# First attention's loop: SyncE issues the next output weights' loads and the kept operands' write in front of the second stacking

## The reference, cut to what matters

```
x = x + 0.5 * ffn(layernorm(x))          # router, top 2 of 8 experts of rank 16
x = x + attention(layernorm(x))          # latent attention, 32 heads
x = x + 0.5 * ffn(layernorm(x))
```

```
q = rms_norm(x @ wq_a.T, q_norm_w) @ wq_b.T        # 128 plain + 64 rotated columns a head
kv = x @ wkv_a.T                                   # 128 latent + 64 rotated, shared by the heads
kv_up = rms_norm(kv_c, kv_norm_w) @ wkv_b.T        # k_nope and v of each head
scores = (q_nope . k_nope + q_pe . k_pe) * scale   # causal
out = softmax(scores) @ v                          # all heads, then out @ wo.T
```

## Time and profile before

| | |
|---|---|
| median of 3 timed runs | 2177.68 us (2177.6 to 2181.52) |
| profiled execution | 2180.48 us |
| its span, first to last instruction | 2178.7 us |
| granted TensorE clock, mean | 0.998 |
| PE busy | 2123.7 us (97%) |
| DVE, ACT, POOL busy | 1585.4, 1371.0, 1247.1 us (73%, 63%, 57%) |
| iteration of the first attention's loop | 60.1 us |
| queue q1 | 244.64 MB, 36.7% of 16 engines' span |

### The profile page before, as it was taken

The page is one execution under the profiler, slowest core; times in us unless marked ns, Lnnn a source line. Parts: engine busy times, 40 slices in busy tenths (PEclk is TensorE's granted clock), DMA queues, the critical chain, the costliest instruction groups (busy, mean ns, idle before and its releaser), DMA issues.

```text
span 2178.7 us, 44641 instructions
## 1 busy us (share of the span) xinstructions
PE 2123.7 (97%) x11548; PEld 1802.3 (83%) x11548; DVE 1585.4 (73%) x3415; ACT 1371.0 (63%) x3561; POOL 1247.1 (57%) x1643
## 2 busy tenths in 40 slices
PE   8989999999999999999899999999999999999998
PEld 7977888888888888888688978888888888888877
DVE  7667777777777777778787667777777777777777
ACT  6556666666666666666665566666666666666664
POOL 5336666666776666666554355555555555555543
PEclk9999999999999999999999999999999999999999
DMA  4034444443334444445423133333333333333331
GB/s 164 19 79 142 137 146 136 145 127 120 104 119 138 146 135 142 146 155 165 147 79 121 52 101 115 114 114 114 114 114 114 114 114 114 114 114 114 111 98 78
DMA packets 221201, 258.02 MB, mean 118 GB/s; under 512 B 145872, under 2 KB 174672, under 8 KB 219088
## 3 DMA queue, kind: packets, MB, share of 16 engines
q1 hardware_dynamic: 216528, 244.64, 36.7%
q10 hardware_dynamic: 4608, 12.58, 1.7%
HBM read 127.14 MB, written 79.69 MB: 95 GB/s over the span
## 4 chain that ended last, share of the span: by engine, by line
PE 65%; DMA 10%; POOL 9%; issue 5%; DVE 4%; ACT 3%; SPq 3%; POOLq 0%; ACTq 0%; DVEq 0%
PE ps L890 50%; DMA stage<-in_wo 7%; PE ps L969 5%; PE ps L1302 4%; PE ps L1246 2%; DMA arena<-arena 2%; PE ps L916 1%; DMA stage<-stage 1%; POOL arena L2703 1%; PE ps L904 1%; SPq L781 1%; POOL stage L2704 1%; POOL stage L2698 1%; ACT arena L1463 1%; ACT stage L1837 1%
## 5 line engine op out<-in xcount | busy, mean ns | idle before, releaser
L2412 DVE TENSOR_TENSOR xacc<-ps,xacc 128x512 f32<-128x512 f32 x896 | 603.0, 686 | 190.9 <-PE ps L890 177.1
L2021 DVE TENSOR_TENSOR arena<-ps,arena 128x512 fp32r<-128x512 f32 (+4 forms) x744 | 425.3, 577 | 202.0 <-ACT arena L1463 201.7
L890 PE MATMUL ps<-arena,extra 128*128 128x512 f32 x1920 | 522.6, 401 | 5.7 <-DVE xacc L2412 5.4
L1828 ACT ACTIVATE stage<-ps,negmax 128x128 f32<-128x128 f32 (+6 forms) x512 | 260.2, 508 | 339.3 <-DVE negmax L2391 332.7
L1463 ACT ACTIVATE arena<-ps 128x512 fp32r<-128x512 f32 (+4 forms) x744 | 369.3, 506 | 137.9 <-PE ps L890 57.3
L890 PE MATMUL ps<-zT,arena 128*128 128x512 f32 (+1 forms) x1746 | 446.3, 400 | 1.9 <-DVE arena L2021 1.0
L890 PEld LDWEIGHTS ps<-arena,extra 128*128 128x128 f32 x1920 | 341.7, 188 | 88.8 <-DVE xacc L2412 17.9
L890 PEld LDWEIGHTS ps<-zT,arena 128*128 128x128 f32 x1746 | 317.6, 189 | 68.8 <-ACT stage L1463 1.3
L2716 POOL TENSOR_TENSOR extra<-extra_plain,extra 128x256 fp32r<-128x256 f32 (+1 forms) x256 | 223.4, 875 | 164.8 <-ACT extra L1463 164.4
L890 PE MATMUL ps<-arena 128*128 128x512 f32 x960 | 262.1, 408 | 14.2 <-POOL arena L2716 7.9
L890 PE MATMUL ps<-keyT,arena 128*128 128x192 f32 (+5 forms) x1152 | 265.7, 339 | 3.6 <-ACT stage L1828 3.6
(11 more groups left out here) (129 smaller groups left out, 3117.9 us busy)
## 6 DMA issues: line engine op xcount, KB each, us to landing
kept_b<-arena SPq DMA_DIRECT2D x16, 3584.0 KB, 11.2
arena<-kept_b SPq DMA_DIRECT2D x112, 512.0 KB, 6.1
arena<-arena SPq DMA_DIRECT2D x128, 128.0 KB, 3.0
stage<-in_wo SPq DMA_DIRECT2D x32, 512.0 KB, 13.2
stage<-stage SPq DMA_DIRECT2D x248, 64.0 KB, 2.0
extra<-arena SPq DMA_DIRECT2D x120, 128.0 KB, 3.0
kept_q<-arena SPq DMA_DIRECT2D x16, 768.0 KB, 11.1
arena<-kept_q ACTq DMA_DIRECT2D x32, 384.0 KB, 6.6
```

What stands on the lines that cost most here:

```text
L890: last = nc.tensor.matmul(dst, w, m, start=start and n == 0, stop=stop and n == len(passes) - 1, skip_group_check=skip)
L1828: nc.scalar.activation(prob[u][:, poff(u, i):poff(u, i) + w], bank_s(i)[:, 0:w], ACT.Exp, bias=negmax[:, k % 2, i:i + 1], accum_out=rowsum ...
L2021: return nc.vector.tensor_tensor(dst, src, part.bitcast(F32), ALU.subtract)
L2412: nc.vector.tensor_tensor(xs, bank_y(k, j), xs, ALU.add).then_inc(y_added, 1)
```

## The change

Inside `body`, in the first attention (p = 0), the block of four moves from behind the second stacking to a place in front of it, directly behind the swap for `pe0`; in the block, `load_wo(g + 1)` moves in front of `kept(g - 1)` and `keep_b(g)`. In the groups with early loads the fourth early load now comes behind the block. The last group's `kept(g)` stays at the end. Nothing is computed in another way, and `first_body` and the second attention stay as they are.

```diff
                     swap_halves()
+                if p == 0 and not last:
+                    landed_wqn(g + 1)
+                if p == 0:
+                    split_b(g)
+                    if not last:
+                        load_wo(g + 1)
+                    kept(g - 1)
+                    keep_b(g)
                 if early:
                     load_early(g, 3)
                 if not last:
                     stack_halves(turns(p, g, 1) + 1, 0, 4 * slot_n(p, g, 2))
-                if p == 0:
-                    if not last:
-                        landed_wqn(g + 1)
-                    split_b(g)
-                    kept(g - 1)
-                    keep_b(g)
-                    if not last:
-                        load_wo(g + 1)
-                    else:
-                        kept(g)
+                if p == 0 and last:
+                    kept(g)
```

## The result

The changed kernel takes 2187.26 us (median of 6 runs, 2184.82 to 2190.23) against 2178.82 us of the kernel before (6 runs): a ratio of 1.0039, 95% interval 1.0027 to 1.0052. It is slower by 8.4 us, 5.9 to 11.3 by the interval. A second set, beside its parts, gave 2189.49 against 2179.79, 1.0041 (1.0028 to 1.0054). I had forecast a slower kernel, by 5 us. The median of the kernel before stands at 2178.82 with six runs, where the forecast started from the 2177.68 of three.

What follows compares the result with a forecast made beforehand. TensorE, busy 97%, was taken as the bound; 13 x (0.9 - 0.75) = +2.0, next to last iteration +2.05, last +1 gave +5 us: 2182.7 against 2177.68, with 8 in 10 from 2168 to 2194.

Steps and rivals of the forecast that it cites:

- The bound and the old stop: TensorE, 97% busy, stops 0.75 us per iteration for the output weights; removing this gives -10.5 us.
- The number of old stops: Stops of TensorE at the output weights' products: 14 taken as removed, -10.5 us together (bounds -6.7 and -12.7).
- When the block starts: On SyncE, first DMA at 705.9, 0.3 us after DVE's last low part; through by 709.1, stacking's issue not delayed.
- The loads: Output weights on SyncE's queue: asked for 10.3 us earlier, landing in 4.1 to 5.3 us, by 713; wanted at 729.
- The stacking behind write and loads: Stacking transfers land at 723.75, after the next first scores want them; TensorE stops 0.9 us (bounds 0.25 and 1.25).
- the first body's order: First body's loads, stacking, then write take 17.2 us together; from 705.9 that ends at 723.1.
- the loop's sum: In the loop, write and loads need 15.3 us, stacking alone 2.9; together 18.2 us, ending at 724.1.
- The early groups: Last two iterations with early loads of x: +2.05 us in the next to last, +1 in the last.
- What moved along: After the stacking, GpSimd's 2.72 us wait for the swap shrinks and it starts 2 to 3 us earlier; counted as nothing.
- The stop moves and nothing is left: Rival: stacking lands at 723.1, -3.5 us, 2174; chance 0.15, including a stop just as long as the old one.
- Faster: Rival: stacking passes or shares engines with the write, landing before 722.85; -10.5 us, 2167; chance 0.22.
- Clearly slower: Rival: write at loop pace and slower 256 B pieces, stacking landing at 724.5; 2193 us; chance 0.18.

Runs made afterwards that it cites:

- the other two executions: Profiled executions of the changed kernel again (2189.49 us) and of the change in groups 1 to 13 only (2184.18 us), with periods 60.59 and 60.46 us.
- the loop alone: The change in groups 1 to 13 only, groups with early loads of x in the old order: 2184.18 us against 2180.05 of the kernel before, ratio 1.0022.
- the early groups alone: The change in groups 14 and 15 only, groups 1 to 13 in the old order: 2184.89 us against 2179.79 of the kernel before, ratio 1.0020.

## Why the prediction was right

- **The bound and the old stop.** 0.75 us was worked out from the gap (0.48), the overlap (0.16) and the longer first product (0.11). The periods give 0.77. The weight port's 12.7 us over 14 alone would have said 0.91, the array's 6.7 over 14 would have said 0.48.
- **The number of old stops: one too many.** Of the 14 of the earlier trace rows one stands in group 0, ahead of the loop, and group 15 didn't wait for its output weights before. 13 stops were removed, so the removed term is 13 x 0.75 = 9.75 us and not 10.5, and the next to last iteration's term should have been 2.8, without the 0.75 taken off.
- **When the block starts.** 0.3 us after the low part, and the stacking's issue still on time: both as stated.
- **The loads.** They land in 4.4 to 6.3 us for the 4.1 to 5.3 reckoned. The stop at line 1246 is gone.
- **The stacking behind write and loads: the right mechanism, a term sized too small.** Taken 0.9 us, measured 1.18 by the periods; between the bounds 0.25 and 1.25. I had put the landing midway between the first body's order (17.2 us from the first issue) and the loop's sum (18.2). In the iteration shown this came true: it landed 17.83 us after the first issue (711.33 to 729.16) for the 17.85 taken, and the scores began 18.26 us after the low part where they begin 17.41 after it in the kernel before (705.58 to 722.99), 0.85 us late for the 0.9. As idle time of the array that is 0.71, since the overlap of 0.16, which the stop takes away, doesn't show in it. But this is one of the shorter gaps. The longest and the shortest of the 13:

```profile
245.28 0.39 PE L1280 MATMUL ps<-keyT,arena 128*128 128x256 f32 x1 [1.21 <-DMA arena<-arena]
426.66 0.38 PE L1280 MATMUL ps<-keyT,arena 128*128 128x256 f32 x1 [0.54 <-DMA arena<-arena]
```

Their mean is 12.1/13 = 0.93, so the landing is on average 0.2 us later than I took, nearer to the loop's sum. The other 0.1 us is a term that I had counted in the old stop and left out of the new one: the first product behind a stop takes 0.38 us for 0.28. 0.93 + 0.16 + 0.10 = 1.19. The same sum with the mean gap of the other two executions (1.00 and 0.88) gives 1.26 and 1.14 where their periods give 1.26 and 1.13. With 1.18 the 13 groups cost 13 x (1.18 - 0.77) = 5.3 us instead of 2.0.
- **The early groups: about the right size, in part by another path.** Forecast +3.05. The whole less the loop alone is 3.1 us by the medians, the early groups alone 5.1. DVE's wait was put at 3.4 us and was 3.72; in group 15 it was put at 1 and was 0.67. PE's stop of 2.8 us was to be a wait for the late stacking; it was a wait for DVE at line 890, of 2.26 us, and the stacking landed within it. That the sum still fits is in part luck: the forecast had too long a stop there and took a stop off it that didn't exist.
- **What moved along.** GpSimd's wait for the first swap fell from 2.72 us to 0.34, as expected, for nothing:

```profile
678.40 1.27 POOL L2698 TENSOR_TENSOR stage<-stage,pos_tab 128x512 f32<-128x512 f32 x1 [0.34 <-POOL stage L2693]
```

- **Not foreseen:** the issues of the stacking grow from 2.7 to 10 us. It cost next to nothing: with six sevenths of the write in front the issue still took 9.1 us and 0.12 us of the stop were left. SyncE waits for the landing anyway.
- **The rivals.** "The stop moves and nothing is left" took the first body's 17.2 us for the loop; the loop is nearer 18. "Faster" took a place in the queue for harmless. It holds for each half of the block alone, where 17.4 us are enough, and for six sevenths of the write. "Clearly slower" (2193 us, write at its slow pace) is near what the order write, loads, stacking does: 2193.17, 13.1 us above its before where the rival had 15.7.

The loads alone in front, 0.56% under before, move only the transfer whose landing PE waited for. The write alone in front (0.60%) and six sevenths of it (0.44%) have intervals that overlap with it, so none of the three is shown to be the fastest.

## What to carry to other kernels

A transfer that is moved forward in a queue is paid for by whatever has a deadline behind it: add up the time of all that now stands in front, from the moment that releases the first, and hold it against the time until the consumer asks. Move the transfer that is waited for, and leave the large write that nobody waits for behind the small one with the deadline. The price of a stop is more than the idle time of the array: the overlap that it takes away and the longer first product belong to it, in the old stop as in the new. The period of a loop that has neither gives the price of each, here to about 0.1 us from one execution. And look where each of the counted stops lies before all of them are booked as won.

## What the runs showed of the hardware that was not expected

- The time that SyncE needs to issue a DMA grew with what stood in front of it in the queue: in the iteration shown the third of the four stackings took 6.62 us to issue behind the loads and the write, 0.64 us with the loads alone. With the write alone in front, the four took 5.12 us; with the loads alone, 2.72 us, as before.
- The same 3.5 MB write lands in 11.2 us when the output weights' 1.2 MB of HBM reads stand right behind it in the queue (before, and write then loads), and in 10.4 to 10.5 us when they don't (the two kernels with only one of the two in front), although the reads land after it (727.3 for the values' weights, 727.0 for the write, by the earlier trace rows). The cause wasn't looked for.
